# Second attention's projection back as three products of rounded parts and rests, queries and keys in one buffer

## The reference, cut to what matters

```python
y  = _L1_cond_ref(x, zX, zY, zR, 1, 1)        # second differences along both axes, and y(1-y)
xn = seq * rsqrt(mean(seq * seq, -1) + eps) * g_norm
q, k, v = split(xn @ W_qkv)                    # 16 heads of 64, n = 256 per batch element
q, k = rotated(q), rotated(k)                  # segments of 128 rows, 16 memory keys and values each
attn = softmax(where(mask, q @ k.T / 8, -1e30))
out = (attn @ v) @ W_out                       # 1024 -> 256: the projection back
x = x + out
```

## Time and profile before

| what | value |
|---|---|
| runs | 2506.01 us median of 3 (2502.82 to 2506.65) |
| profiled execution's own time | 2517.34 us |
| its span, first to last instruction | 2515.6 us |
| busy PE, PEld | 2365.0 us (94%), 2100.1 us (83%) |
| busy DVE, ACT, POOL | 1848.3 us (73%), 1257.4 us (50%), 1020.0 us (41%) |
| granted clock of PE, mean | 0.975 of 2.4 GHz |

### The profile page before, as it was taken

How to read it: one execution, slowest core, us unless ns; L and a number is a source line. 1 busy time by engine, 2 the same in 40 slices (tenths; PEclk the granted TensorE clock), 3 DMA queues, 4 the chain that set the end, 5 groups by cost and what they waited for, 6 DMA issues and landing times.

```text
span 2515.6 us, 54476 instructions
## 1 busy us (share of the span) xinstructions
PE 2365.0 (94%) x18880; PEld 2100.1 (83%) x18880; DVE 1848.3 (73%) x5113; ACT 1257.4 (50%) x3774; POOL 1020.0 (41%) x1074
## 2 busy tenths in 40 slices
PE   4899999999988799999999999799999999999999
PEld 3677887878866688888888887699999999999999
DVE  5777777777777766676666664468878888888866
ACT  1666666666654355555555555324325555555422
POOL 4545545455443544454454454123322222222063
PEclk7899999999988899999999999899999999999999
DMA  3321211212120222112212212221126677777433
GB/s 114 104 51 45 58 45 41 51 45 58 35 85 9 65 51 55 46 46 55 49 43 55 51 43 52 56 68 41 37 61 210 231 238 227 231 230 240 139 105 121
DMA packets 153079, 225.71 MB, mean 90 GB/s; under 512 B 54294, under 2 KB 123174, under 8 KB 142054
## 3 DMA queue, kind: packets, MB, share of 16 engines
q1 hardware_dynamic: 143942, 203.56, 27.7%
q0 software_dynamic: 8864, 18.66, 2.8%
HBM read 159.32 MB, written 27.16 MB: 74 GB/s over the span
## 4 chain that ended last, share of the span: by engine, by line
PE 70%; DVE 10%; issue 8%; ACT 7%; POOL 3%; DMA 1%; SPq 0%; POOLq 0%; ACTq 0%; DVEq 0%
PE bank L55 55%; PE bank L136 7%; PE bank L1239 2%; PE bank L336 2%; ACT P L1430 2%; PE bank L363 1%; PE bank L1280 1%; ACT Ph L618 1%; DVE xe L881 1%; ACT PTh L630 1%; ACT L1478 1%; DVE xe L884 1%; POOL P L1703 1%; PE bank L446 1%; DVE Ph L767 1%
## 5 line engine op out<-in xcount | busy, mean ns | idle before, releaser
L1430 ACT ACTIVATE P<-P,mx 128x144 f32<-128x144 f32 x512 | 206.3, 404 | 344.6 <-DVE mx L1540 344.6
L55 PE MATMUL bank<-xD_hi,w1e_lo 128*128 128x256 f32 x880 | 253.8, 288 | 0.8 <-issue 0.8
L55 PE MATMUL bank<-xD_lo,w1e_hi 128*128 128x256 f32 x880 | 249.0, 283 | 1.2 <-issue 1.2
L55 PE MATMUL bank<-w2e_lo,hrD_hi 128*128 128x256 f32 x880 | 249.1, 283 | 0.8 <-issue 0.7
L55 PE MATMUL bank<-w2e_hi,hrD_lo 128*128 128x256 f32 x880 | 249.0, 283 | 0.8 <-issue 0.8
L2508 POOL DMA_INDIRECT xE<-d_y,ixs x78 | 111.1, 1425 | 341.5 <-PE bank L136 314.7
L55 PE MATMUL bank<-w2e_hi,hrD_hi 128*128 128x256 f32 x880 | 249.1, 283 | 0.4 <-issue 0.4
L55 PE MATMUL bank<-xD_hi,w1e_hi 128*128 128x256 f32 x880 | 248.9, 283 | 0.4 <-issue 0.4
L1073 POOL TENSOR_TENSOR xe<-xe 128x704 f32<-128x704 f32 (+3 forms) x64 | 88.4, 1381 | 395.4 <-DVE xe L886 395.2
L2123 ACT ACTIVATE hD<-bank,b1E 128x256 f32<-128x256 f32 x312 | 128.5, 472 | 199.4 <-PE bank L55 185.1
L2194 DVE CAST hrD_hi<-hD 128x512 fp32r<-128x512 f32 x284 | 121.1, 426 | 118.7 <-ACT hD L2123 106.6
(11 more groups left out here) (318 smaller groups left out, 7822.4 us busy)
## 6 DMA issues: line engine op xcount, KB each, us to landing
w1raw<-in_ew SPq DMA_DIRECT2D x39, 1024.0 KB, 6.0
w2raw<-in_ew SPq DMA_DIRECT2D x39, 1024.0 KB
K<-Kn SPq DMA_DIRECT2D x256, 72.0 KB, 2.1
Q<-Qn SPq DMA_DIRECT2D x256, 64.0 KB, 2.0
d_ys<-oE SPq DMA_DIRECT2D x39, 256.0 KB
d_rot<-QK SPq DMA_DIRECT2D x16, 512.0 KB, 2.9
Rs<-d_rot SPq DMA_DIRECT2D x64, 128.0 KB, 4.2
b2E<-in_eb SPq DMA_DIRECT2D x39, 128.0 KB, 3.4
```

Source lines behind the costliest of these rows:

```text
L55: inst = e.matmul(out, l, r, start=k == 0, stop=k == len(pairs) - 1)
L1430: inst = e.activation(P1[t % 2][:, n, :], P1[t % 2][:, n, :], ACT.Exp, bias=mx1[t % 2][:, 2 * g + sg:2 * g + sg + 1], scale=-1.0, accum_ou ...
```

## The change

- The projection back (`back`) uses `matmuls3` on pairs OT1 and wo1: 24 fp32r products per call where there were 8 plain f32 ones.
- OT1's rounded part is written by ACT for both banks (two copies per half of the heads, c_O1 counts twice). The rest is made by DVE, which subtracts it from the banks (`out_low`, two subtractions per half where there was one copy). `values` and `back` wait for DVE's count alone. In DVE's order it stands behind the rotation of its step, where the copy stood ahead of it.
- wo1 is loaded into the second buffer of the values, right behind pmv, and split in four parts by ACT and DVE at the end of steps 1, 2, 3 and 5 of body 0 (`split_back`). The first copy into that buffer waits for the last part.
- Q1 and K1 have one buffer. A stack of a half waits until the scores of that half of the element before have been taken.
- `normalize` is parted: its first instruction (`sums`, L1616) stays at the start of step 4, the rest (L1619, L1622 and both L1626) goes to the end of step 5. `x_low` goes from the end of step 5 to the end of step 7, `x_high` from step 5 to step 6, ahead of the copy of the values there.

```diff
@@ tiles
-        Q1, K1, V1 = [tile("Q10", 8, 256)], [tile("K10", 8, 288)], [tile("V10", 2, 1024)]
+        Q1, K1, V1 = tile("Q1", 8, 256), tile("K1", 8, 288), [tile("V10", 2, 1024)]
...
-        OT1, wo1, pmv = tile("OT1", 8, 256), tile("wo1", 8, 256), tile("pmv", 8, 128)
+        rawo = V1[1].rearrange("p s (f n) -> p (s f) n", n=256)
+        OT1, wo1, pmv = pair("OT1", 8, 256), pair("wo1", 8, 256), tile("pmv", 8, 128)
@@ sync_c
-                if b >= 2:
-                    e.wait_ge(p_S1, 8 * (b - 1))
                 for half in range(2):
                     e.wait_ge(g_r1, 8 * b + 4 * half + 4)
+                    if b >= 1:
+                        e.wait_ge(p_S1, 8 * (b - 1) + 4 * half + 4)
...
                         e.dma_start(pmv, a["pmv"]).then_inc(l_pm[0], 16)
-                if b == 0:
-                    e.dma_start(wo1, a["wo1"]).then_inc(l_co, 16)
+                        e.dma_start(rawo, a["wo1"]).then_inc(l_co, 16)
@@ pe_c, values
-                    e.wait_ge(c_O1, t // 4)
                     e.wait_ge(v_O1, t // 4)
@@ pe_c, back
-                    e.wait_ge(c_O1, 2 * b + 2)
                     e.wait_ge(v_O1, 2 * b + 2)
...
                     if b == 0:
-                        e.wait_ge(l_co, 16)
-                matmuls(e, halves(1)[:, d, :], [(wo1[:, f, d * 128:d * 128 + 128], OT1[:, f, :])
-                                                for f in range(8)]).then_inc(p_back, 1)
+                        e.wait_ge(v_w1, 10)
+                matmuls3(e, halves(1)[:, d, :], [
+                    (cut(wo1, lambda x: x[:, f, d * 128:d * 128 + 128]), cut(OT1, lambda x: x[:, f, :]))
+                    for f in range(8)]).then_inc(p_back, 1)
@@ act_c, out_copy and values_copy
-                e.activation(OT1[:, 4 * half:4 * half + 4, 0:128], quarters(4), ACT.Copy).then_inc(c_O1, 1)
+                for sg in range(2):
+                    e.activation(OT1[0][:, 4 * half:4 * half + 4, 128 * sg:128 * sg + 128], quarters(4 + sg), ACT.Copy
+                                 ).then_inc(c_O1, 1)
...
+                elif b:
+                    e.wait_ge(v_w1, 10)
+            def split_back(f):
+                e.wait_ge(l_co, 16)
+                e.activation(wo1[0][:, f:f + 2, :], rawo[:, f:f + 2, :], ACT.Copy).then_inc(c_w1, 1)
@@ act_c, loop
-                    if s == 5:
+                    if s == 6:
                         x_high(entering(b))
...
+                    if b == 0 and s in (1, 2, 3, 5):
+                        split_back(2 * (1, 2, 3, 5).index(s))
@@ dve_c
-                e.tensor_copy(OT1[:, 4 * half:4 * half + 4, 128:256], quarters(5)).then_inc(v_O1, 1)
+                for sg in range(2):
+                    at = (slice(None), slice(4 * half, 4 * half + 4), slice(128 * sg, 128 * sg + 128))
+                    e.wait_ge(c_O1, t // 4 * 2 + sg + 1)
+                    inst = e.tensor_tensor(OT1[1][at], quarters(4 + sg), OT1[0][at].bitcast(F32), ALU.subtract)
+                inst.then_inc(v_O1, 1)
...
+            def split_back(f):
+                e.wait_ge(c_w1, 7 + f // 2)
+                e.tensor_tensor(wo1[1][:, f:f + 2, :], rawo[:, f:f + 2, :],
+                                wo1[0][:, f:f + 2, :].bitcast(F32), ALU.subtract).then_inc(v_w1, 1)
@@ dve_c, loop
                     if s == 4:
-                        normalize(entering(b))
+                        sums(entering(b))
                         add_back(b - 1)
...
                     maxima(t + 1)
-                    if s % 4 == 0:
-                        out_copy(t - 1)
                     if s == 0:
                         rotate(b + 1, 0)
...
                     if s == 4:
                         rotate(b + 1, 4)
+                    if s % 4 == 0:
+                        out_low(t - 1)
...
                     if s == 5:
+                        normalize(entering(b))
+                    if s == 7:
                         x_low(entering(b))
...
+                    if b == 0 and s in (1, 2, 3, 5):
+                        split_back(2 * (1, 2, 3, 5).index(s))
```

More of the change, by code:

```diff
@@ L1146, in program @@
         tile("space1", 120)
-        Q1, K1, V1 = [tile("Q10", 8, 256)], [tile("K10", 8, 288)], [tile("V10", 2, 1024)]
+        Q1, K1, V1 = tile("Q1", 8, 256), tile("K1", 8, 288), [tile("V10", 2, 1024)]
         PmT1 = [tile(f"PmT1{i}", 128) for i in range(2)]
-        Q1.append(tile("Q11", 8, 256))
         V1.append(tile("V11", 2, 1024))
-        K1.append(tile("K11", 8, 288))
-        OT1, wo1, pmv = tile("OT1", 8, 256), tile("wo1", 8, 256), tile("pmv", 8, 128)
+        rawo = V1[1].rearrange("p s (f n) -> p (s f) n", n=256)
+        OT1, wo1, pmv = pair("OT1", 8, 256), pair("wo1", 8, 256), tile("pmv", 8, 128)
         PT1 = [tile(f"PT1{i}", 2, 2, 128) for i in range(2)]
@@ L1199, in stack @@
                         at, j, steps = 64 * (i % 2) + 32 * eo, 2 * half, slice(4 * half + i // 2, 4 * half + i // 2 + 3, 2)
-                        for dst, src in ((Q1[b % 2], Qn), (K1[b % 2], Kn)):
+                        for dst, src in ((Q1, Qn), (K1, Kn)):
                             e.dma_start(dst[at:at + 32, steps, :], src[32 * i:32 * i + 32, j:j + 2, eo, :]
@@ L1239, in scores @@
                         inst = e.matmul(bank[g][:, 144 * sg:144 * sg + 144],
-                                        Q1[par][64 * g:64 * g + 64, s, 128 * sg:128 * sg + 128],
-                                        K1[par][64 * g:64 * g + 64, s, 144 * sg:144 * sg + 144], start=True, stop=True)
+                                        Q1[64 * g:64 * g + 64, s, 128 * sg:128 * sg + 128],
+                                        K1[64 * g:64 * g + 64, s, 144 * sg:144 * sg + 144], start=True, stop=True)
                 inst.then_inc(p_S1, 1)
@@ L1558, in copy_turned, with out_low @@
                               ).then_inc(v_PT1, 1)
-            def out_copy(t):
+            def out_low(t):
                 if not 0 <= t < 8 * B or t % 4 != 3:
                     return
-                b, half = t // 8, t // 4 % 2
-                e.wait_ge(p_PV1, t + 1)
-                if b:
-                    e.wait_ge(p_back, 2 * b)
-                else:
-                    e.wait_ge(v_w1, 6)
-                e.tensor_copy(OT1[:, 4 * half:4 * half + 4, 128:256], quarters(5)).then_inc(v_O1, 1)
+                half = t // 4 % 2
+                for sg in range(2):
[3 more added lines that the diff above has]
+                inst.then_inc(v_O1, 1)
             def rotate(b, n):
@@ L1608, in field, with sums @@
                                        ).then_inc(v_t7, 1)
-            def normalize(b):
+            def sums(b):
                 if not 0 <= b < B:
@@ L1617, in normalize @@
                                        op0=ALU.add, op1=ALU.mult).then_inc(v_rn, 1)
+            def normalize(b):
+                if not 0 <= b < B:
+                    return
                 e.wait_ge(v_rn, 2 * b + 1)
@@ L1658, in dve_c @@
                     if b == -3 and s == 5:
+                        sums(0)
                         normalize(0)
@@ L1811, in program @@
             "h", "x", "f2", "R", "yD", "lg", "marks", "rk", "slot", "tab", "cb", "w2E"))
-        c_wD, v_wD, WD = c_w1, v_w1, 6
+        c_wD, v_wD, WD = c_w1, v_w1, 10
         WE = WD + 3
```

## The result

The changed kernel takes 2535.08 us (median of 4 runs, 2534.26 to 2537.35), the kernel before 2506.24 (4 runs, 2502.82 to 2506.65). The ratio is 1.0114, 95% interval 1.0102 to 1.0126: slower by 28.8 us, where 12 were forecast. The direction was right, the size was not, and the time lies outside the range (2498 to 2524).

A forecast was written before the change was run, and what follows sets the result against it. PE was taken to bound the second attention (busy 666 of 687 us). 13 x 0.68 = 8.8, plus 3.0 - 0.2 + 0.1 + 0.2, gave +12 us: 2518 us against the median of 2506.0, range 2498 to 2524.

The forecast's parts named there:

- What PE gains: Each `back` falls from 3.55 to 3.0 us: gain 0.54 per call, 1.08 per body, 17.3 for 32 calls.
- Step 0: ACT's two result copies precede the values' copy that PE's second projection waits for: PE held 0.48 us longer.
- Step 3: Second `back` ends 0.6 us early, but PE's values in step 4 wait for PmT behind ACT's root: 0.12 early.
- Step 4, out_low in DVE's way: DVE's two subtractions delay the values: a wait on DVE replaces one on ACT, 0.05 us early.
- Step 5, the normalization: Moved instructions and POOL's wait for each other: 2.57 us, PE's transposes of step 6 0.68 late, in 13 bodies 8.8.
- One buffer: Q and K stacks of about 10 us, covered by 5 us before and 11 behind: price 0.
- The end, +0.1 for body 15 and +0.2 behind it: Body 15: values 1.2 us late against -1.08, +0.1. Last `back`: two copies and a subtraction more, +1.25 against -1.08, +0.2.
- PE's gaps drop its clock: Part of a rival: PE's 1 us gaps drop its clock now and then; 13 x 0.4 = +5, 2524 us; chance 0.10.
- Body 0, +3.0: Four splits ahead of inversions: step 3 hidden by the root, steps 1, 2 and 5 1 us each; bounds 0 and 5.
- The level: +12 us on the profiled execution's 2517.3, set against the median of 2506.0, 11.3 lower, gives 2518 us.

The follow-up runs named there:

- e11: e7 with ACT's root behind the turned copies of step 3 and DVE's sums behind `add_back`: 2507.99 us, 0.9993 of before.
- e15: Changed kernel with two of the three products in the projection back: 2515.94 us (1 run), body 46.61.
- e4: Kernel before with only the change's order (normalization parted, x_high in step 6, x_low in step 7): 2523.94 us, 1.0024 of before.
- e6: Changed kernel with POOL's combine of projection 6 moved behind its normal product of step 6: 2520.03 us, 1.0050 of before.
- e8: Kernel before with one buffer of queries and keys, nothing else of the change: 2510.64 us, 1.0010 of before.
- e14: Changed kernel with only 40 added products that nobody reads, where PE waits at the attention's end: 2523.34 us, 1.0064 of before.
- e1: Changed kernel with the whole normalization back in step 4, x_high and x_low back in step 5: 2539.39 us, 1.0079 of before.
- e2: Changed kernel with ACT's last values' copy ahead of its two copies of the result in step 0: 2539.36 us, 1.0078 of before.
- e5: Changed kernel run once more, unchanged, on another chip: 2533.79 us, 1.0107 of before.
- e10: Changed kernel with each of wo1's four splits in body 0 done twice, on ACT and DVE: 2538.92 us (1 run), body 0 55.7.
- e9: Kernel before run once more, unchanged: 2510.19 us, 0.9999 of before.
- e16: Kernel before with added products (8, 8 and 4) at three places at the attention's end: 2510.19 us, 1.0012 of before.
- e3: Changed kernel with the rest of the normalization at the end of step 6 and x_high in step 7: 2524.89 us, 1.0022 of before.
- e7: Changed kernel with the edits of e3 and e2 together: 2513.94 us, 1.0028 of before.
- e13: e11 with 40 added products at the end and wo1's four splits moved to steps 4 and 5 of body 0: 2491.03 us, 0.9934 of before.
- second pair: Traces of two later runs of the same two kernels, e9 (before) and e5 (changed): span longer by 27.0 us.
- e17: Kernel before (plain products, two buffers, no splits, no added products) in the order of e13: 2490.96 us, 0.9929 of before.

## Why the prediction was right or wrong

- **What PE gains**: 0.54 us per call forecast, 0.51 measured (3.04). Right. The quarter that the Trainium skill's four passes would give (FP8 and Floating Point Precision, TensorE Precision Notes) did not come: it is 14%, near the 15% that the rows had said.
- **Step 0**: 0.48 forecast, 0.48 measured, on the wait named. Right.
- **Step 3**: "0.12 early, not 0.6". The steps say -0.59 and then +0.59. Right, and shown by e11 and e15.
- **Step 4, out_low in DVE's way**: a wait of 0.30 on DVE's PT in step 5. Right. That the normalization's leaving step 4 does not help holds only with `out_low` there: alone it brings 0.83 (e4).
- **Step 5, the normalization**: 2.57 us forecast, 2.60 measured from 1375.51 to 1378.11; the wait of 1.0 in 13 bodies is there. Right, and shown by e4 and e6. A body is 0.74 longer for 0.68 forecast. (The instructions with two SBUF inputs that moved are four, not three; the two on fa run when POOL is idle, 0.88 us for both.)
- **One buffer**: price 0. Right in the bodies (e8).
- **The end, +0.1 for body 15 and +0.2 behind it, is the step that failed most.** +0.3 was forecast, +3.8 and +9.1 were measured. Two terms were wrong. The chain, at the full clock, costs 2.3: I had the copies and `out_low` in one short step of body 15 (+1.2), and they stand in two. From e8 to e14 step 1 goes from 4.05 to 5.49 us and step 5 from 3.56 to 5.49, the start of the last `back` is 1.2 later, and against it stand 0.6 in each of steps 2 and 3 and 1.1 in the last two calls. And I put PE's clock at nothing. "PE's gaps drop its clock" stood among the rivals, for the full bodies, where it did not happen (granted clock 1.00 before and after; in e1 it did, in two bodies). It happened at the end, where PE had waits of 2.0 to 2.4 us in place of 0.8 to 1.6, and cost 3.7 us in one trace and 7.6 in the other, where before's traces lose 2.2 and 0.8 by it. The rows had a sign of it: the 32 products of the earlier trace rows take 8.54 us behind a wait of 0.84, where two calls of the full bodies take 7.1.
- **The start was left out.** I costed the moved steps in the full bodies and not in body -1, which also holds a normalization, beside rotations and with no scores yet. There the rest of the normalization stands ahead of the last rotation. The timelines of PE just ahead of body 0, before and after:

```profile
852.53 0.47 PE L55 MATMUL bank<-w_hi,xr_lo 128*128 128x512 f32 x1 [0.35 <-DVE tb L1579]
```

```profile
853.95 0.61 PE L55 MATMUL bank<-w_hi,xr_lo 128*128 128x512 f32 x1 [2.23 <-DVE tb L1587]
```

  That it is the order, e4 (before's products) and e1 (the changed kernel's products, old order) show:

```profile
855.61 0.63 PE L55 MATMUL bank<-w_hi,xr_lo 128*128 128x512 f32 x1 [2.24 <-DVE tb L1579]
```

```profile
850.36 0.47 PE L55 MATMUL bank<-w_hi,xr_lo 128*128 128x512 f32 x1 [0.34 <-DVE tb L1587]
```

  The 1.9 us recur: 2.2 also in e2, e5, e6, e10, e14 and e15, 0.3 to 0.4 in e8, e9 and e16, and no such wait in e3 and e7. Behind this wait the clock fell to half in six of the eight traces that have it, the changed kernel's first among them, and the way from there to body 0 took 8.3 to 8.4 us for 6.9; in e5 and e10 it did not. What lies ahead of the wait scatters by up to 2.7 us (before, e8, e9 and e16). So it is chance that both pairs give the same 3.0: in the first it is 1.9 + 1.5 - 0.5, in the second 1.9 + 1.1.
- **Body 0, +3.0, was mis-sized**: 5.2. The normalization's collision costs 1.1 in step 6 (e4, without a split, has 6.22 for 5.13), and `out_low` 0.57 in step 5, where PE waits for DVE's PT; the sum had both in 13 bodies and forgot them in this one, where no wait for ACT covers the second (step 5 is 5.08 before, 5.90 in body 10). The other 3.5 are left to the splits: 0.60 and 0.76 in steps 2 and 3, which e13 gives back by their place, 0.6 in step 6 behind the normalization (6.81), and 1.6 in step 4. Of that 1.6, 1.15 is the longer wait for PmT (3.04 for 1.89), the rest half clock, which scatters: e8's step 4 has no split and takes 10.20. The forecast hid the split of step 3 behind the root; it stands behind it in ACT's queue, and DVE's inversion waits for it.
- **The level**: I subtracted the 11.3 us by which the profiled execution stood above the median, as if both kernels' traces did so. The changed kernel's trace is of an execution at its median. The 8 us behind the attention in before's first trace (918.0 for 910.1) were that execution's.

Of the 15 us between forecast and second pair, 8.8 are the end (2.0 the chain and 6.8 the clock), 3.0 the start, 2.3 body 0, 0.9 what follows the attention. What sets the waits of PE put down to "issue" is open: with the filler they are gone in the changed kernels (0.3 us or less) and not in before, so it is not PE's being busy as such. That they come from where the instructions lie was not tried. The first trace of before, at 2517.34 us and with 9.1 us of them, looks like those from the chip where before takes 2517.88; on which chip it was taken is not on record.

## What to carry to other kernels

Cost a moved step in every body that it runs in, the short first and last ones first: there the covers are missing, and behind waits of 2 us PE's clock fell to 1.2 GHz in most traces here (granted clock 0.73 and 0.85 over the end in the changed kernel's two). Before a faster product is written for the bound engine, move what its gain would run into: here the order alone gave 0.7% (e17), and with the products on top it was 0.7% again (e13). Ask of every DVE instruction with two SBUF inputs what POOL does beside it.

## What the runs showed that was not expected

- Forty products that compute nothing made the end of the attention 7.6 us shorter (e14 against e5, granted clock 1.00 for 0.73).
- PE stands behind the attention with nobody named that it waits for, 0 to 12.9 us in all, in 0 to 14 places. Chips differ: where before takes 2517.9, they are 9 us and more. On e11 (on the timeline of PE) one alone is 4.25:

```profile
1661.00 0.28 PE L55 MATMUL bank<-hrD_hi,f_lo 128*128 128x256 f32 x1
1665.53 0.37 PE L55 MATMUL bank<-hrD_lo,f_hi 128*128 128x256 f32 x1 [4.25 <-issue]
```

- The same kernel's end took 45.8 and 49.7 us in two executions whose longest waits are the same (2.4 and 2.0 us): the clock makes such a stretch uncertain by several us, while bodies 1 to 14 together agree to 0.1.
